# Reading back the expert results: three tiles later in the row queue, and VectorE's last sums held until every scatter has landed

## The chip, the cores and the metric

The kernel runs on one core of one Trainium2 chip. The metric is the device time in microseconds of one execution, lower being better. The core has TensorE (PE in the profile, with weight loads as PEld), VectorE (DVE), ScalarE (ACT), GpSimd (POOL) and SyncE (SP). SP and GpSimd issue the transfers here: SP plain ones, GpSimd those that gather or scatter rows by a list of addresses.

## The reference

A macaron block on 4096 tokens of width 256 (2 x 2048): half a mixture-of-experts step, attention with a convolution ahead of it, and half a mixture-of-experts step again with the same weights. The change touches only the last part.

```
x = x + 0.5 * _L0_ffn_ref(_layernorm(x), gate_up_proj, down_proj, router_w)
x = x + _L0_attn_ref(_layernorm(x), ...)
x = x + 0.5 * _L0_ffn_ref(_layernorm(x), gate_up_proj, down_proj, router_w)

# _L0_ffn_ref: 8 experts, hidden width 176, each token goes to its best two
probs = softmax(h @ router_w.T); vals, idx = top_k(probs, 2); vals = vals / vals.sum()
for each expert:  y = silu(h @ gate.T) * (h @ up.T) @ down.T
                  acc = acc + combine_weight[token, expert] * y
```

## The kernel before

Tokens lie in 32 token tiles of 128. For the expert step, each token's two copies are sorted by expert, and the sorted rows fill 71 expert tiles of 128 rows (`SLOT_TILES`), some of them padding. In the second expert step (`R[1]`) the five engines each run a loop over the expert tiles `s`:

- SP (`load_rows`, L615) loads the 128 rows of tile `s` (129 KB) from DRAM into a ring of four places in `yg`. It issues this when tile `s - 4` has been turned by TensorE and VectorE has read the addresses of tile `s - 4` from the ring (`rowsT`, `dest`).
- TensorE turns the rows (L1842), multiplies by gate and up weights (L1855), turns the hidden rows (L1866, L1867) and multiplies by the down weights (L1875 to L1879). It works two tiles deep: in step `s` it turns tile `s + 1`, does gate and up of `s`, turns hidden `s - 1` and does down of `s - 2`.
- VectorE and ScalarE split values into high and low parts between these; ScalarE copies the result out of PSUM (`y_sb`, L861), and VectorE computes where each row goes (`y_dest`, L1391).
- GpSimd (`send_sums`, L767) scatters the 128 result rows to DRAM (`y_rows`), where the two results of one token are neighbours. The semaphores `st0` to `st3` count the scatters that landed.

Then come the last sums. Token tile `t` becomes x + w0 * y0 + w1 * y1. VectorE does 20 token tiles, two operations each (`last_sum`, L1152, both inputs and the output in SBUF). ScalarE and TensorE do the other 12 (`BY_ACT`, L1064, L1745, L1747, L1069). SP stores the result, two token tiles at a time, in 16 stores of 256 KB (`store_sums`, L637).

The results must be read back from `y_rows`. All results of the first 20 token tiles (`AHEAD`) are in expert tiles below 47 (`AHEAD_FROM`), whatever the routing, because attention's tokens were sorted in two parts. So SP reads those 20 token tiles (256 KB each, `load_ahead`, L623, into buffers that nothing uses any more) while the expert loop still runs: one ahead of the row load of each of the expert tiles 52 to 70, and the last one behind it. Ahead of the first it waits for the scatters below tile 47. The remaining 12 token tiles are read in six transfers of 512 KB into `w_lo` (`load_sums`, L631), when all 71 scatters have landed. SP works its queue strictly in order: a wait ahead of one transfer holds all that stand behind it.

Of the kernel before, what the change touches and what calls it, by code (L numbers as in the profile page):

```python
# [40 lines left out]
SLOT_TILES = (TOPK * TOKENS + E * (P - 1)) // P  # L41
# [31 lines left out]
TAIL_TURN = TILES + 1  # L73
AHEAD_FROM = (TOPK * EARLY_BLOCKS * P + E * (P - 1)) // P
AHEAD = EARLY_BLOCKS
AHEAD_AT = AHEAD_FROM + 5
EARLY_ROUNDS = EARLY // 4


# [27 lines left out]
def macaron_kernel(nc, x, conv_w, conv_b, wq, wk, wvT, wo, bq, bk, bo, proj_w, proj_b, gupT, dpT, rwT,  # L107
                   out, h_dram, y_dram):
    ctx = ExitStack()
    with ctx:  # L110
# [131 lines left out]
        RING = 4  # L242
# [94 lines left out]
        R = [dict() for _ in range(2)]  # L337
# [96 lines left out]
        def in_ring(u):  # L434

            return (SLOT_TILES - u + RING - 1) // RING
# [120 lines left out]
        @block.sync  # L557
        def _(sp):
            for c in range(CHUNKS):
                sp.dma_start(x_view[:, c * CHUNK:(c + 1) * CHUNK, :], x_rows[:, c * CHUNK:(c + 1) * CHUNK, :]  # L560
                             ).then_inc(x_in[c], 16)
                if c == 0:
                    sp.dma_start(rw_sb[:, :], rwT).then_inc(rw_in, 16)
            sp.wait_ge(made, 4)
            for k in range(2):
                for dst, src in w_loads[k]:
                    sp.dma_start(dst, src, allow_slow_non_contiguous=True).then_inc(w_in[k], 16)

            def store_first(groups):
                for g in groups:  # L570
                    sp.wait_ge(first["normed"], GROUP * (g + 1))
                    sp.dma_start(h_dram[g * GROUP * P:(g + 1) * GROUP * P, :].rearrange("(i p) d -> p i d", p=P),
                                 h_rings[g]).then_inc(first[f"stored{g}"], 16)

            store_first((0, 1))
            for dst, src in loads:
                sp.dma_start(dst, src, allow_slow_non_contiguous=True).then_inc(loaded, 16)
            store_first((2, 3))

            pad_regs = [sp.alloc_register(f"pad_at{e}") for e in range(E)]  # L580

            def fill_pad(e):
                if e == 0:
                    sp.wait_ge(T["pads_at"], 1)
                    sp.load(pad_regs, pad_i[0:1, :])
                at = sp.snap(pad_regs[e], min_val=e * REGION, max_val=e * REGION + TOKENS)
                sp.dma_start(h_regions[bass.ds(at, P), :], pad_rows[:, :]).then_inc(T["pads"], 16)

            def load_rows(L):
                r = R[L]  # L590
                regs = [sp.alloc_register(f"rows_at{u}") for u in range(8)]
                for first in range(0, TABLE_TILES, 8):
                    if first in (0, EARLY):
                        sp.wait_ge(T["row_table"], 1 + first // EARLY)
                    sp.load(regs, row_i[0:1, first:first + 8])
                    if first == 0:
                        sp.wait_ge(T["combined"], TILES)
                        for q in range(GROUP):
                            sp.wait_ge(T[f"sent{q}"], 32 * len(range(q, EARLY_BLOCKS, GROUP)))
                    if first == EARLY:  # L600
                        for q in range(GROUP):
                            sp.wait_ge(T[f"sent{q}"], 32 * TILES // GROUP)
                        sp.wait_ge(T["pads"], 16 * E)
                        sp.wait_ge(T["dummies"], 16 * SPARE_TILES)
                    for n in range(min(8, SLOT_TILES - first)):
                        s = first + n
                        if FIRST_PAD <= s < FIRST_PAD + E:
                            fill_pad(s - FIRST_PAD)
                        at = sp.snap(regs[n], min_val=0, max_val=E * REGION + (SPARE_TILES - 1) * P)
                        if AHEAD_AT <= s < AHEAD_AT + AHEAD:  # L610
                            load_ahead(s - AHEAD_AT)
                        if s >= RING:
                            sp.wait_ge(r["rowsT"], s + 1)
                            sp.wait_ge(r["dest"], s - RING + 1)
                        sp.dma_start(rows_in[L][:, s % RING, :], h_regions[bass.ds(at, P), :]  # L615
                                     ).then_inc(r[f"g{s % RING}"], 16)

            def load_ahead(t):

                if t == 0:  # L620
                    for u in range(RING):
                        sp.wait_ge(R[1][f"st{u}"], 16 * len(range(u, AHEAD_FROM, RING)))
                sp.dma_start(ahead_in[t], y_tokens[:, t, :]).then_inc(y_in(t // 2)[0], 16)  # L623

            def load_sums(L):
                for t in range(SLOT_TILES - AHEAD_AT, AHEAD):
                    load_ahead(t)
                for u in range(RING):
                    sp.wait_ge(R[L][f"st{u}"], 16 * in_ring(u))
                for g in range(AHEAD // 2, TILES // 2):  # L630
                    sp.dma_start(y_pairs(g), y_tokens[:, 2 * g:2 * g + 2, :]).then_inc(y_in(g)[0], 16)  # L631

            def store_sums():
                for g in range(TILES // 2):
                    sp.wait_ge(final, sum(t not in BY_ACT for t in range(2 * g + 2)))
                    after(sp, final_act, sum(t in BY_ACT for t in range(2 * g + 2)))
                    sp.dma_start(out_rows[:, 2 * g:2 * g + 2, :], x_view[:, 2 * g:2 * g + 2, :]).then_inc(written, 16)  # L637
                sp.wait_ge(written, 16 * (TILES // 2))

            def store_y(L):  # L640
                r = R[L]

                def store(s, u):
                    sp.wait_ge(r["y_sb"], s + 1 + 2)
                    sp.dma_start(y_dram[bass.ds(s * P, P), :], y_sb[:, u, :]).then_inc(r[f"st{u}"], 16)

                with sp.Fori(0, SPARE_TILES) as j:
                    for u in range(RING):
                        store(RING * j + u, u)
                    sp.dma_start(h_regions[bass.ds(j * P + E * REGION, P), :], pad_rows[:, :]  # L650
                                 ).then_inc(T["dummies"], 16)
                with sp.Fori(0, SLOT_TILES // RING - SPARE_TILES) as j:
                    for u in range(RING):
                        store(RING * j + u + RING * SPARE_TILES, u)
                for s in range(SLOT_TILES // RING * RING, SLOT_TILES):
                    store(s, s % RING)

            sp.wait_ge(loaded, 16 * len(loads))
            sp.wait_ge(first["tokens"], 1)
            sp.dma_start(conv_sb, conv_w).then_inc(loaded, 16)  # L660
            store_y(0)
            for p in range(TILES // 2):
                sp.wait_ge(T["qk"], p + 1)
                sp.dma_start(swapped[W:2 * W, p % 2, :], qk[p % 2][0:W, :]).then_inc(T["swapped"], 16)
                sp.dma_start(swapped[0:W, p % 2, :], qk[p % 2][W:2 * W, :]).then_inc(T["swapped"], 16)
            load_rows(1)
            load_sums(1)

            store_sums()
# [431 lines left out]
        def _(v):  # L1101
            st = Steps(v, dve)
# [38 lines left out]

            def last_sum():
                by_dve = [t for t in range(TILES) if t not in BY_ACT]
                for pair in zip(by_dve[0::2], by_dve[1::2]):
                    done = []
                    for k in range(TOPK):
                        for n, t in enumerate(pair):
                            if k == 0:
                                v.wait_ge(*y_in(t // 2))
                            else:  # L1150
                                v.wait_ge(dve, done[n])
                            ins = v.scalar_tensor_tensor(out=x_tile(t),  # L1152
                                                         in0=y_block(t)[:, k * D:(k + 1) * D],
                                                         scalar=wts[:, k, t:t + 1], in1=x_tile(t),
                                                         op0=ALU.mult, op1=ALU.add)
                            if k == 0:
                                st.did(ins)
                                done.append(st.n)
                            else:
                                ins.then_inc(final, 1)  # L1160
# [1050 lines left out]
```

## Time and profile before

| | |
|---|---|
| time, median of 3 runs | 756.57 us (755.98 to 757.07) |
| the profiled execution's own time | 754.7 us |
| its span in the profile | 752.9 us |
| PE busy | 668.6 us (89%) |
| DVE busy | 522.3 us (69%) |
| ACT busy | 489.9 us (65%) |
| POOL busy | 379.5 us (50%) |
| transfers | 85.50 MB, mean 114 GB/s |

Busy shares are means over stages with different limits. The expert loop of the second step and the last sums, the last 190 us or so, are the part in which the changed lines run; there one reads which engine waits for what, from the timeline and the chain of waits.

### The profile page before, as it was taken

How to read it: one execution, taken by the hardware profiler on the slowest of the kernel's cores; microseconds unless marked ns; L12 is line 12 of the kernel's file. 1: busy time of each engine (PE TensorE's matmuls, PEld its weight loads, DVE VectorE, ACT ScalarE, POOL GpSimd, SP SyncE). 2: the span in 40 equal slices, each digit the busy share in tenths (PEclk: the TensorE clock that was granted, in tenths of full speed). 3: DMA queues.
4: the chain of work that ended last, by engine and by line, in shares of the span. 5: the costliest groups of instructions: out<-in, count | busy, mean ns of one | idle time of the engine just before them, and what ended most of it. 6: DMA issues, size and time to landing. Idle time of an engine off the chain costs nothing. (4 is left out here: it accounts for less than half of the span.)

```text
span 752.9 us, 18893 instructions
## 1 busy us (share of the span) xinstructions
PE 668.6 (89%) x5168; PEld 593.7 (79%) x5169; DVE 522.3 (69%) x1831; ACT 489.9 (65%) x1702; POOL 379.5 (50%) x418
## 2 busy tenths in 40 slices
PE   3999799999997699998898989878688999989974
PEld 3986699999994578887787878767467999979953
DVE  6587566666666467777878777858768677756762
ACT  5775566666664278888877878768444666656653
POOL 4200644444434545666887877563645444434450
PEclk9999899999999689999999999999968999999998
DMA  9930345544442211111222222010223644457619
GB/s 307 311 125 1 109 142 148 146 128 131 130 113 84 84 37 36 41 53 52 78 65 65 66 71 63 30 64 16 93 86 111 180 134 128 128 171 231 190 62 334
DMA packets 60584, 85.50 MB, mean 114 GB/s; under 512 B 10192, under 2 KB 46547, under 8 KB 60500
## 3 DMA queue, kind: packets, MB, share of 16 engines
q1 hardware_dynamic: 47492, 49.73, 21.8%
q0 software_dynamic: 13008, 34.69, 14.8%
q8 instruction: 47, 0.77, 0.5%
q14 instruction: 37, 0.30, 0.2%
HBM read 45.77 MB, written 37.44 MB: 111 GB/s over the span
## 5 line engine op out<-in xcount | busy, mean ns | idle before, releaser
L1855 PE MATMUL CC<-w_hi,turned_parts 128*128 x568 | 176.7, 353 | 2.5 <-DVE turned_parts L1378 2.5
L750 POOL DMA_INDIRECT shared<-h_rows,tok_i x71 | 69.9, 984 | 117.1 <-issue 59.1
L767 POOL DMA_INDIRECT y_rows<-shared,y_dest x71 | 77.7, 1095 | 80.0 <-DVE y_dest L1391 57.5
L1855 PEld LDWEIGHTS CC<-w_hi,turned_parts 128*128 128x128 f32 x568 | 106.8, 195 | 3.3 <-issue 3.2
L843 ACT ACTIVATE shared<-CC 128x176 f32<-128x176 f32 x142 | 45.2, 318 | 78.0 <-PE CC L1855 72.4
L1855 PE MATMUL CC<-w_lo,turned_parts 128*128 x284 | 93.9, 331 | 0.0
L959 ACT ACTIVATE pr<-SS,nmax 128x128 f32<-128x128 f32 x256 | 90.4, 400 | 0.0
L783 POOL TENSOR_TENSOR pr<-pr,prec 128x1024 f32<-128x1024 f32 x31 | 58.9, 1901 | 51.2 <-DVE prec L1614 49.9
L1372 DVE TENSOR_TENSOR shared<-shared,CC 128x176 f32<-128x176 f32 x142 | 47.9, 338 | 50.0 <-ACT shared L843 28.7
L814 POOL DMA_INDIRECT h_regions<-h_store,dest x64 | 65.0, 1015 | 32.7 <-issue 17.2
L791 POOL DMA_INDIRECT yg<-y_rows,slot_i x64 | 62.7, 979 | 34.5 <-DMA y_rows<-shared 15.5
L861 ACT ACTIVATE shared<-SS 128x256 f32<-128x256 f32 x142 | 54.6, 385 | 29.7 <-issue 14.8
L959 ACT ACTIVATION_READ_ACCUMULATOR pr<-SS,nmax 128x1 f32 x256 | 61.7, 241 | 0.0
L950 ACT ACTIVATE shared<-CC 128x512 f32<-128x512 f32 x64 | 34.7, 594 | 33.5 <-PE CC L1997 30.7
L1855 PEld LDWEIGHTS CC<-w_lo,turned_parts 128*128 128x128 f32 x284 | 55.8, 197 | 0.0
L1875 PE MATMUL SS<-w_hi,turned_parts 128*128 x142 | 52.4, 369 | 1.0 <-DVE turned_parts L1385 0.7
L1378 DVE TENSOR_TENSOR turned_parts<-A,turned_parts 128x256 fp32r<-128x256 f32 x68 | 28.9, 425 | 26.4 <-ACT turned_parts L849 26.0
L1378 DVE TENSOR_TENSOR turned_parts<-B,turned_parts 128x256 fp32r<-128x256 f32 x74 | 31.4, 424 | 21.6 <-ACT turned_parts L849 17.8
L1989 PE MATMUL SS<-shared 64*128 64x128 f32 x256 | 38.3, 292 | 5.8 <-DVE shared L1489 4.4
L1584 DVE TENSOR_REDUCE nmax<-SS 128x8 f32<-128x1024 f32 x32 | 39.0, 1219 | 4.6 <-PE SS L1989 4.6
L1989 PEld LDWEIGHTS SS<-shared 64*128 64x128 f32 x256 | 32.1, 194 | 11.2 <-issue 3.0
L1878 PE MATMUL SS<-w_lo,turned_parts 112*128 x142 | 40.7, 287 | 0.0
(404 smaller groups left out, 2108.9 us busy)
## 6 DMA issues: line engine op xcount, KB each, us to landing
yg<-h_regions SPq DMA_DIRECT2D x71, 129.0 KB
y_rows<-shared SPq DMA_DIRECT2D x71, 128.0 KB
x_sb<-in_x_dram SPq DMA_DIRECT2D x8, 512.0 KB, 9.7
out_dram<-x_sb SPq DMA_DIRECT2D x16, 256.0 KB, 6.6
w_lo<-y_rows SPq DMA_DIRECT2D x6, 512.0 KB, 4.2
w_lo<-in_gupT_dram SPq DMA_DIRECT2D x2, 1408.0 KB, 12.4
shared<-tile_oh SPq DMA_DIRECT2D x32, 64.0 KB
h_regions<-pad_rows SPq DMA_DIRECT2D x15, 129.0 KB
```

What stands on the lines that cost most here:

```text
L750: pool.indirect_dma_start(out=rows[:, s % RING, 0:D], out_offset=None, in_=h_dram[:, :], in_offset=bass.IndirectOffsetOnAxis(ap=tok_i[:, s ...
L767: pool.indirect_dma_start(out=y_dram[0:TOPK * TOKENS, :], out_offset=bass.IndirectOffsetOnAxis(ap=y_dest[:, s:s + 1], axis=0), in_=y_sb[:, ...
L783: pool.tensor_tensor(pr[:, q, :, :], pr[:, q, :, :], prec[:, q, :].unsqueeze(2).to_broadcast([P, NH, P]), ALU.mult).then_inc(t["norm"], 1)
L791: pool.indirect_dma_start(out=yg[:, q, k, :], out_offset=None, in_=y_dram[:, :], in_offset=bass.IndirectOffsetOnAxis(ap=slot_i[:, b, k:k + ...
L814: pool.indirect_dma_start(out=h_regions[:, :], out_offset=bass.IndirectOffsetOnAxis(ap=dest[:, q, k:k + 1], axis=0), in_=hr[:, q, :], in_o ...
L861: a.activation(y_sb[:, u % RING, :], SS[:, 512 * (u % 2):512 * (u % 2) + D], ACT.Copy).then_inc(r["y_sb"], 1)
L959: e = a.activation(pr[:, u % 2, h, :], SS[:, h * P:(h + 1) * P], ACT.Exp, bias=nmax[:, u % 2, h:h + 1], accum_out=psums[:, u % 2, h:h + 1])
L1372: v.tensor_tensor(hid[:, p, 0:H], gate[:, p, :], CC[:, 512 * p + H:512 * p + GU], ALU.mult).then_inc(r["hid"], 1)
L1378: v.tensor_tensor(rowsT_lo[:, p, :], rows_turned(r, u), rowsT_hi[:, p, :].bitcast(F32), ALU.subtract).then_inc(r["rowsT_lo"], 1)
L1855: i = pe.matmul(CC[:, 512 * (u % 2):512 * (u % 2) + GU], rows_part[:, u % 2, c * P:(c + 1) * P], weights, start=(n == 1), stop=(n == 3 * DC))
L1875: pe.matmul(acc, hidA_hi[:, u % 2, :], w_hi[:, at_a], start=True, stop=False)
L1989: x = pe.matmul(SS[:, at_h * P:(at_h + 1) * P], heads[lo:lo + KD, m % 2 * 2 + m // 2, :], key_of(i, h % 2), start=False, stop=True, skip_g ...
```

## The change

The 20 reads ahead begin at the row load of expert tile 55 instead of 52, and are spread over the 16 row loads that are left: one ahead of most, two ahead of four of them (of tiles 58, 62, 66 and 70). None is left for after the loop. VectorE's first last sum also waits until all 71 scatters have landed. What is waited for ahead of the first read ahead (the scatters below tile 47) is as before.

```
-AHEAD_AT = AHEAD_FROM + 5
+AHEAD_AT = AHEAD_FROM + 8
...
-                        if AHEAD_AT <= s < AHEAD_AT + AHEAD:
-                            load_ahead(s - AHEAD_AT)
+                        if s >= AHEAD_AT:
+                            for t in ahead_with(s - AHEAD_AT):
+                                load_ahead(t)
...
+            def ahead_with(n):
+
+                steps = SLOT_TILES - AHEAD_AT
+                return range(n * AHEAD // steps, (n + 1) * AHEAD // steps)
+
...
             def load_sums(L):
-                for t in range(SLOT_TILES - AHEAD_AT, AHEAD):
-                    load_ahead(t)
                 for u in range(RING):
                     sp.wait_ge(R[L][f"st{u}"], 16 * in_ring(u))
...
             def last_sum():
                 by_dve = [t for t in range(TILES) if t not in BY_ACT]
+                for u in range(RING):
+                    v.wait_ge(R[1][f"st{u}"], 16 * in_ring(u))
                 for pair in zip(by_dve[0::2], by_dve[1::2]):
```

The first place is SP's queue in the expert loop. L615 is the row load of an expert tile (the ISA row ahead of it carries its waits), L623 the read ahead. Before, the queue around the row loads of tiles 51 to 54 reads so:

```order
L615 ISA [waits r1_dest,r1_rowsT]
L615 DMA yg<-h_regions 128x258
L623 DMA conv_qk_hi<-y_rows 128x512 [waits r1_st2,r1_st3,r1_st1,r1_st0]
L615 ISA [waits r1_dest,r1_rowsT]
L615 DMA yg<-h_regions 128x258
L623 DMA conv_qk_lo<-y_rows 128x512
L615 ISA [waits r1_dest,r1_rowsT]
L615 DMA yg<-h_regions 128x258
L623 DMA pr<-y_rows 128x512
L615 ISA [waits r1_dest,r1_rowsT]
L615 DMA yg<-h_regions 128x258
```

Now the row loads have the line L616 and the reads ahead L629; around the row loads of tiles 54 to 58 it reads:

```order
L616 DMA yg<-h_regions 128x258
L629 DMA conv_qk_hi<-y_rows 128x512 [waits r1_st2,r1_st3,r1_st1,r1_st0]
L616 ISA [waits r1_dest,r1_rowsT]
L616 DMA yg<-h_regions 128x258
L595 TENSOR_LOAD row_i
L629 DMA conv_qk_lo<-y_rows 128x512
L616 ISA [waits r1_dest,r1_rowsT]
L616 DMA yg<-h_regions 128x258
L629 DMA pr<-y_rows 128x512
L616 ISA [waits r1_dest,r1_rowsT]
L616 DMA yg<-h_regions 128x258
L629 DMA conv_v<-y_rows 128x512
L629 DMA pr<-y_rows 128x512
```

The wait on the scatters stood ahead of the row load of tile 52 and stands ahead of that of tile 55; the row loads of 52, 53 and 54 have moved in front of it.

The second place is VectorE's program where the expert loop ends (L1384 and L1385 are its last two operations for an expert tile) and the last sums begin. Before:

```order
L1384 TENSOR_TENSOR turned_parts<-F,turned_parts 128x128 [waits r1_hidT_hi]
L1385 TENSOR_TENSOR turned_parts<-F,turned_parts 48x128
L1152 SCALAR_TENSOR_TENSOR x_sb<-conv_qk_hi,wts,x_sb 128x256 [waits y_in0]
L1152 SCALAR_TENSOR_TENSOR x_sb<-conv_qk_lo,wts,x_sb 128x256 [waits y_in0]
L1152 SCALAR_TENSOR_TENSOR x_sb<-conv_qk_hi,wts,x_sb 128x256 [waits dve]
```

And now:

```order
L1390 TENSOR_TENSOR turned_parts<-F,turned_parts 128x128 [waits r1_hidT_hi]
L1391 TENSOR_TENSOR turned_parts<-F,turned_parts 48x128
L1158 SCALAR_TENSOR_TENSOR x_sb<-conv_qk_hi,wts,x_sb 128x256 [waits r1_st3,r1_st2,y_in0,r1_st1,r1_st0]
L1158 SCALAR_TENSOR_TENSOR x_sb<-conv_qk_lo,wts,x_sb 128x256 [waits y_in0]
L1158 SCALAR_TENSOR_TENSOR x_sb<-conv_qk_hi,wts,x_sb 128x256 [waits dve]
```

Only the first sum has new waits, on the four scatter semaphores; all 40 sums stand behind it. ScalarE's, TensorE's and GpSimd's programs are the same instruction for instruction.

## Rows read from the trace of the kernel before

**Rows 1.** The chain that ended last, in the expert loop: start us, us, what.

```profile
662.99 7.10 issue
670.21 0.34 SPq L623
...
671.05 2.85 DMA yg<-h_regions
```

**Rows 2.** Timeline of PE, the turns of tiles 51, 52, 53, 55 and 70.

```profile
668.22 0.38 PE L1842 MATMUL B<-ident,yg 128*128 128x128 f32 x2
673.95 0.44 PE L1842 MATMUL A<-ident,yg 128*128 128x128 f32 x2 [3.56 <-DMA yg<-h_regions]
676.63 0.63 PE L1842 MATMUL B<-ident,yg 128*128 128x128 f32 x2
...
681.59 0.38 PE L1842 MATMUL B<-ident,yg 128*128 128x128 f32 x2
...
712.04 0.38 PE L1842 MATMUL A<-ident,yg 128*128 128x128 f32 x2
```

**Rows 3.** Busy time by stretch: window, PE, PEld, DVE, ACT, POOL; PEclk, DMA share, GB/s.

```profile
640.00:660.00 20.00, 19.98 (x148) 19.41 (x147) 14.10 (x50) 13.22 (x50) 9.60 (x11) 1.00 0.43 133
660.00:680.00 20.00, 16.44 (x112) 16.09 (x111) 10.79 (x38) 10.12 (x38) 7.41 (x8) 0.91 0.54 174
680.00:700.00 20.00, 19.90 (x149) 19.49 (x148) 14.15 (x49) 13.23 (x50) 9.34 (x10) 1.00 0.80 240
```

**Rows 4.** Timeline of POOL: the scatters of tiles 46, 69 and 70.

```profile
667.76 0.98 POOL L767 DMA_INDIRECT y_rows<-shared,y_dest  x1 [1.03 <-DVE y_dest L1391]
...
718.99 1.07 POOL L767 DMA_INDIRECT y_rows<-shared,y_dest  x1 [0.60 <-issue]
720.37 8.01 POOL L767 DMA_INDIRECT y_rows<-shared,y_dest  x1 [0.30 <-issue]
```

**Rows 5.** Timeline of DVE and of ACT: last sums (ACT: copy of tile 18).

```profile
717.53 0.48 DVE L1152 SCALAR_TENSOR_TENSOR x_sb<-conv_qk_hi,wts,x_sb 128x256 f32<-128x256 f32 x1
...
727.04 0.47 DVE L1152 SCALAR_TENSOR_TENSOR x_sb<-hT_sb,wts,x_sb 128x256 f32<-128x256 f32 x1
729.96 0.38 ACT L1069 ACTIVATE x_sb<-B 128x256 f32<-128x256 f32 x1 [0.29 <-PE B L1747]
733.43 0.48 DVE L1152 SCALAR_TENSOR_TENSOR x_sb<-w_lo,wts,x_sb 128x256 f32<-128x256 f32 x1 [5.92 <-DMA w_lo<-y_rows]
...
741.74 1.27 DVE L1152 SCALAR_TENSOR_TENSOR x_sb<-w_lo,wts,x_sb 128x256 f32<-128x256 f32 x3 [1.51 <-DMA w_lo<-y_rows]
```

**Rows 6.** The chain that ended last, in the tail.

```profile
720.37 9.16 DMA y_rows<-shared,y_dest
...
745.12 0.38 ACT x_sb L1069
```

**Rows 7.** Timeline of DVE and of POOL at 75 us.

```profile
75.33 2.88 DVE L1237 TENSOR_TENSOR w_lo<-w_lo,w_hi 128x960 fp32r<-128x960 f32 x4
...
75.34 3.85 POOL L750 DMA_INDIRECT shared<-h_rows,tok_i  x1 [43.09 <-DVE tok_i L1271]
```

**Rows 8.** SP's queue, timeline: row load of tile 70, and the tail.

```profile
705.64 0.33 SPq L615 DMA_DIRECT2D yg<-h_regions  x1
...
729.67 3.05 SPq L631 DMA_DIRECT2D w_lo<-y_rows  x6
732.76 16.10 SPq L637 DMA_DIRECT2D out_dram<-x_sb  x16
```

**Rows 9.** Busy time by stretch in the tail, columns as in rows 3.

```profile
731.00:739.00 8.00, 3.18 (x14) 2.11 (x12) 3.79 (x10) 3.18 (x8) 0.00 (x0) 1.00 0.94 334
...
743.00:751.00 8.00, 2.09 (x9) 1.46 (x7) 0.01 (x1) 0.77 (x2) 0.00 (x0) 0.93 1.09 382
```

**Rows 10.** DMA queue: packets, MB, share; issues and us to landing, 715 to 753.

```profile
q1 hardware_dynamic: 5984, 7.34, 54.6%
...
out_dram<-x_sb SPq DMA_DIRECT2D x16, 256.0 KB, 6.6
```

## The prediction

> **What bounds the kernel now.** I read the chain of waits first, because two places in it are no work of any engine. The first is in the expert loop: 7.10 us without an instruction from 662.99, then SP's first read ahead at 670.21, then the row load of tile 52 at 671.05, which lands 2.85 us later [rows 1]. That is SP standing ahead of the first read ahead until the scatter of tile 46 has landed, with the row load of tile 52 behind it. The timeline of TensorE shows what it costs. Tile 52 should be turned 2.0 us after tile 51, and is turned 5.73 us after it, with TensorE idle for 3.56 us on the row load [rows 2]. The window around it has TensorE busy for 16.44 of 20 us, where its neighbours have 19.98 and 19.90; its granted clock is 0.91 instead of 1.00 [rows 3]. So outside this stall TensorE bounds the loop, at one tile per 2.03 us: (712.04 - 681.59) / 15 [rows 2].
>
> The second is behind the loop. The scatter of tile 69 occupies GpSimd for 1.07 us, that of tile 70 for 8.01 us, from 720.37 to 728.38 [rows 4]. It lands 9.16 us after its start [rows 6], and only then, at 729.67, does SP issue the first read into w_lo [rows 8]. In the same time VectorE does its sums on the data read ahead without a gap, from 717.53 to 727.51, and then idles 5.92 us [rows 5]. From 731 on the transfers are the bound: 334 GB/s up to 739 and 382 GB/s from 743 to 751, at a busy share of 0.94 and 1.09, with every compute engine mostly idle [rows 9]. The traffic there is 7.34 MB [rows 10], six reads of 512 KB and 16 stores of 256 KB. At 382 GB/s it is 19.2 us, of the 23.2 between the first issue and the end of the span (752.9 - 729.67).
>
> So two delays are in series. What the loop saves arrives whole at the tail, since all 71 scatters must land before SP goes on.
>
> **Part 1: reads ahead from tile 55.** The wait itself is unchanged: the scatter of tile 46 starts at 667.76 [rows 4] and SP is released at 670.21 [rows 1], 2.45 us later, in the new kernel too. What moves is what stands behind it. The row loads of 52, 53 and 54 go out when their own waits allow. Tile 55 becomes the first one held. A row load that nothing holds goes out 6.4 us before its tile is turned (tile 70: 705.64 [rows 8] and 712.04 [rows 2]). TensorE, without a stall, turns tile 55 at 668.22 + 4 x 2.03 = 676.3, so its row load is wanted at 669.9. SP gets to it at about 671.05, as it got to tile 52 now, and its rows land 2.85 us later, at 673.9 [rows 1]. There are 2.4 us to spare, so the stall is gone and no new one takes its place.
>
> What that is worth: from the turn of tile 51 to that of tile 55 pass 681.59 - 668.22 = 13.37 us now [rows 2], and four steps take 8.1. The gain is 5.3 us: some 3.7 of waiting, and the rest from steps at the lower clock behind the pause (tile 52 to 53 takes 2.68 us), which goes with the pause. The lower bound, if the clock dips anyway, is 3.6 us.
>
> The cost is density. 20 reads of 256 KB go into 16 steps; now 19 go into 19. One read ahead per step raised the busy share of the transfer engines from 0.43 to 0.80 [rows 3], so one is worth 0.37. Five in four steps make 0.43 + 1.25 x 0.37 = 0.89. A step with two has 1.17, which is 0.17 x 2.03 = 0.35 us of backlog, gone in the next two steps. A row load behind two reads ahead instead of one lands some 0.8 us later (256 KB more, at the 334 GB/s of rows 9), so in 3.7 us instead of 2.85, against the 6.4 us that it has. I take 0 us for it, with up to 1.5 us in the range: at four steps the backlog could show on TensorE.
>
> The twentieth read ahead moves from behind the last row load to ahead of it. It is one more issue on SP (0.34 us [rows 1]), with 6.4 us before tile 70 is turned: 0.
>
> **Part 2: VectorE waits for the scatters.** The question is whether the sums are why the last scatter takes 8.01 us. The release fits: the scatter ends at 728.38, 0.87 us behind the end of the sums at 727.51, and 0.98 is what the scatter of tile 46 takes [rows 4, 5]. At 75 us there is a second such case: the first gather starts at 75.34, with VectorE's four subtractions between SBUF tensors from 75.33 to 78.21, and ends at 79.19, 0.98 us behind them [rows 7]. Against it stands the scatter of tile 69, which runs from 718.99 amid the same sums and takes only 1.07 us.
>
> The Trainium skill (SBUF — State Buffer, Who interferes with whom) says that a VectorE instruction with two SBUF inputs contends with a GpSimd instruction that reads SBUF, and that the loser waits for one instruction to end. Read strictly, the scatter would lose one sum of 0.48 us, not 7. The same page's warning on "DVE blocks DMA" says that GpSimd cannot write descriptors while VectorE holds the port pair. By the first the 8 us would have another cause and part 2 would gain nothing; by the second it gains what is worked out below. This trace agrees with the second at two places and with the first at the scatter of tile 69.
>
> I go by the two cases in which GpSimd's operation ends 0.9 to 1.0 us behind VectorE's run. Without the sums, the scatter of tile 70 starts at 720.3 as now (that of 69 sheds 0.1), takes 0.98 us, and lands 2.45 us after its start, as that of tile 46 did [rows 1, 4]. SP then issues the first read of w_lo at 722.7 instead of 729.67: 7.0 us earlier.
>
> VectorE begins its sums at 722.7 instead of 717.53, 5.2 us later, and all 40 stand behind the wait. Each takes 0.40 us (727.51 - 717.53 for 25 of them [rows 5]), so they end at 722.7 + 16 = 738.7, if w_lo is there. It is: the first is needed after 26 sums, at 733.1. ScalarE and TensorE do not wait, and are done with the token tiles read ahead at 730.3, as now [rows 5].
>
> What SP does next: it issues six reads (3.05 us), then stores as token tiles become final, at one per 16 / 16 = 1.0 us from 724.3 on. The reads (3.15 MB at 334 GB/s [rows 9]) fill the transfer engines until 722.7 + 9.4 = 732.1, when eight stores are ready behind them, and at 0.7 us a store (256 KB at 382 GB/s) the backlog lasts until the sums are over. The transfers stay the bound, so the tail behind the first read keeps its 23.2 us: 722.7 + 23.2 = 745.9, against 752.9. Gain 7.0 us. If the first 8 us ran at 382 instead of 334 GB/s, 1.0 us would go too: a gain of 8.0. If stores come too thinly while the reads run, 1 us is lost: a gain of 6.0.
>
> **Sum.** 5.3 + 7.0 = 12.3 us. The profiled execution took 754.7 us with a span of 752.9; less 12.3, 742.4 with a span of 740.6. The median shown is 1.87 us above that execution: 756.57 - 12.3 = 744.3 us.
>
> **Rivals.**
>
> *Only the loop gains.* VectorE's sums cost a scatter no more than one of them, 0.1 to 0.5 us as at tile 69, and the last scatter is slow for another reason, such as something in GpSimd's own end of the loop. (This is what the sentence of the Trainium skill, SBUF — State Buffer, on two SBUF inputs comes to; the trace agrees with it at tile 69 alone.) Then w_lo is read from 729.67 less 5.3 as now, and VectorE starts at that moment too: it ends 16 us later, at 745.7 on the old scale, about when ScalarE is done now (745.5 [rows 6]), so the stores lose little; I give them 0.5 us. 756.57 - 5.3 + 0.5 = 751.8 us. For it speaks the scatter of tile 69; against it two ends that follow VectorE's by 0.9 us. 4 in 100.
>
> *The loop gains little.* The denser reads ahead hold up row loads at the four double steps, or SP's queue backs up. Each lost step is 0.5 to 1 us plus the clock behind it; four of them cost 2 to 4 us. 756.57 - 12.3 + 3 = 747.3 us. For it: a busy share of 0.89 with a backlog at double steps. Against it: 6.4 us of lead against 3.7, and only 0.1 us of TensorE lost in 20 with one read ahead per step [rows 3]. 12 in 100.
>
> *Slower than before.* VectorE's sums become the bound of the tail. Held until 722.7 and then run beside full transfers, they take a time q each; the last store goes out behind the last sum and lands 6.6 us later [rows 10]: 722.7 + 40 q + 6.6 against 752.9 + 5.3. It decides from q = 0.72 us. At q = 0.85 the end is 763.3 less 5.3, that is 758.0, and the time 756.57 + 5.1 = 761.7 us. Against it: the three sums from 741.74, amid full transfers, take 1.27 us, 0.42 each [rows 5]. 2 in 100.
>
> *The change does nothing.* For that SP would have to be held at tile 55 as at 52, with the scatter of tile 46 landing well over 2.4 us later than now, and the last scatter would have to be slow as well: 756.6 us, 1 in 100.
>
> **How the numbers follow.** My forecast has 81 in 100: 744.3, its range from the bounds above. Down: 1.0 us for transfers at full rate, and 1.3 for steps of the loop that are not perfectly even now (TensorE has 19.90 of 20 [rows 3]) and the spread of runs, gives 742.0. Up: 1.5 for the backlog and 1.0 for thin stores give 746.8, or 1.7 if the clock dips anyway; the range goes to 747.8, so that it holds the second rival's centre. What is left out is below 742.0, the worse half of the second rival, and the others. A measurement of this kernel tells a difference from 0.2% (1.5 us) on. Faster by more than that are the forecast and the first two rivals, 0.97 or so; within it the last, 0.01; slower 0.02.
>
> **What the profile of the changed kernel would show.** Part 1: TensorE turns tiles 51 to 55 at an even 2.0 us, the 660 to 680 window has about 19.9 us of TensorE and a clock of 1.00, and the chain has no 7 us gap in the loop. SP's row loads of 52 to 54 come 2 us apart, and the next is near 671. If part 1 is wrong, an idle time of TensorE on the row load stands at tile 55 or behind a double step. Part 2: no scatter above 1.1 us; the last one lands about 2.4 us after its start, and VectorE's first sum and SP's first read of w_lo begin together, at about 717.4 on the new scale (722.7 - 5.3). The transfers then run above 330 GB/s to the end, and VectorE has no idle time on w_lo longer than 2 us. If the scatter takes 8 us again with VectorE idle, my cause is wrong. If the rate between 719 and 728 stays well under 330 GB/s, the stores are too thin and the tail is bound by the sums.

## The result, and the profile after

The changed kernel takes 746.72 us (median of 7 runs, 743.28 to 749.49), against 756.81 us for the kernel before in the same comparison (7 runs). The ratio is 0.9869, with a 95% interval of 0.9837 to 0.9901. Single runs of either kernel scatter by 5 to 6 us. The two profiled executions have spans of 752.9 and 741.1 us, 11.8 us apart; they are one execution each, and that of the changed kernel (743.28 us) is the fastest of its seven, so the difference of the spans says no more about the gain than the medians do. What the two traces are good for is to compare the parts that changed.

The timeline of TensorE shows the turns of tiles 51 to 55 and of tile 70, answering to [rows 2]:

```profile
668.12 0.38 PE L1848 MATMUL B<-ident,yg 128*128 128x128 f32 x2
670.14 0.38 PE L1848 MATMUL A<-ident,yg 128*128 128x128 f32 x2
672.15 0.39 PE L1848 MATMUL B<-ident,yg 128*128 128x128 f32 x2
674.62 0.43 PE L1848 MATMUL A<-ident,yg 128*128 128x128 f32 x2 [0.30 <-issue]
676.70 0.38 PE L1848 MATMUL B<-ident,yg 128*128 128x128 f32 x2
...
707.38 0.38 PE L1848 MATMUL A<-ident,yg 128*128 128x128 f32 x2
```

Tile 51 is turned within 0.1 us of where it was, so from there on the two traces can be laid side by side. Four steps take 8.58 us instead of 13.37. Tile 70 is turned 4.66 us earlier. By stretch, as in [rows 3]:

```profile
660.00:680.00 20.00, 19.70 (x146) 19.30 (x146) 14.14 (x49) 12.98 (x48) 9.25 (x10) 1.00 0.63 194
680.00:700.00 20.00, 19.70 (x148) 19.32 (x147) 14.28 (x50) 13.24 (x50) 9.83 (x10) 1.00 0.89 278
```

TensorE has lost its idle time on the row load and its dip of the granted clock (1.00 instead of 0.91). The transfer engines are denser, 0.89 busy where they were 0.80.

SP's timeline shows where the stall was that it still makes, and the tail ([rows 1, 8]):

```profile
670.21 0.34 SPq L629 DMA_DIRECT2D conv_qk_hi<-y_rows  x1
671.01 0.10 SPq L616 DMA_DIRECT2D yg<-h_regions  x1
...
717.90 3.04 SPq L635 DMA_DIRECT2D w_lo<-y_rows  x6
720.99 16.45 SPq L641 DMA_DIRECT2D out_dram<-x_sb  x16
```

The first read ahead goes out at 670.21, to the hundredth as before. It is now ahead of the row load of tile 55, which goes out at 671.01 and is not missed: tile 55 is turned at 676.70.

GpSimd's last two scatters, and VectorE's last sums ([rows 4, 5]), from the timelines:

```profile
714.33 0.98 POOL L771 DMA_INDIRECT y_rows<-shared,y_dest  x1 [0.60 <-issue]
715.62 0.99 POOL L771 DMA_INDIRECT y_rows<-shared,y_dest  x1 [0.30 <-issue]
```

```profile
717.93 0.48 DVE L1158 SCALAR_TENSOR_TENSOR x_sb<-conv_qk_hi,wts,x_sb 128x256 f32<-128x256 f32 x1 [5.10 <-DMA y_rows<-shared,y_dest]
...
728.63 5.23 DVE L1158 SCALAR_TENSOR_TENSOR x_sb<-w_lo,wts,x_sb 128x256 f32<-128x256 f32 x13
```

The last scatter takes 0.99 us instead of 8.01. VectorE pays for that with 5.10 us of idle time and then does all 40 sums without a gap. By stretch in the tail, as in [rows 9]:

```profile
721.00:727.00 6.00, 6.00 (x26) 4.55 (x27) 6.00 (x16) 5.02 (x13) 0.00 (x0) 1.00 0.92 311
727.00:731.00 4.00, 3.99 (x18) 2.80 (x17) 4.00 (x11) 3.33 (x8) 0.00 (x0) 1.00 1.06 380
731.00:739.00 8.00, 1.48 (x6) 0.97 (x6) 2.85 (x8) 0.77 (x2) 0.00 (x0) 0.85 1.09 383
```

The transfers are full from 727 on. Between 721 and 727 they are not quite, and SP's own waits say why: it now waits 7.3 us in all, 11 times, for VectorE's sums ahead of a store (before: 2.5 us, 5 times).

```profile
SPq L633 <- DMA y_rows<-shared,y_dest: 16.4, 1, 16.4
SPq L641 <- DVE x_sb L1158: 7.3, 11, 1.1
```

### The profile page after: what moved, and what is told of

Its sections match the earlier page's. It is cut to its first block and busy times, and to the rows that moved or that the text cites. A ratio compares the mean times of both kernels' runs of the same rounds, so it can differ in the third digit from the quotient of the medians.

```text
span 741.1 us, 18895 instructions
## 1 busy us (share of the span) xinstructions
PE 663.7 (90%) x5168; PEld 589.3 (80%) x5169; DVE 521.2 (70%) x1831; ACT 488.4 (66%) x1702; POOL 372.2 (50%) x418
## 5 line engine op out<-in xcount | busy, mean ns | idle before, releaser
L771 POOL DMA_INDIRECT y_rows<-shared,y_dest x71 | 70.5, 993 | 75.5 <-DVE y_dest L1397 57.4
L1881 PE MATMUL SS<-w_hi,turned_parts 128*128 x142 | 52.2, 368 | 1.0 <-DVE turned_parts L1391 0.7
L1384 DVE TENSOR_TENSOR turned_parts<-B,turned_parts 128x256 fp32r<-128x256 f32 x74 | 31.3, 423 | 21.1 <-ACT turned_parts L853 17.0
L1384 DVE TENSOR_TENSOR turned_parts<-A,turned_parts 128x256 fp32r<-128x256 f32 x68 | 28.8, 424 | 24.0 <-ACT turned_parts L853 23.7
L1883 PE MATMUL SS<-w_hi,turned_parts 128*128 x142 | 40.4, 285 | 0.0
```

The source lines that it names most:

```text
L771: pool.indirect_dma_start(out=y_dram[0:TOPK * TOKENS, :], out_offset=bass.IndirectOffsetOnAxis(ap=y_dest[:, s:s + 1], axis=0), in_=y_sb[:, ...
L1384: v.tensor_tensor(rowsT_lo[:, p, :], rows_turned(r, u), rowsT_hi[:, p, :].bitcast(F32), ALU.subtract).then_inc(r["rowsT_lo"], 1)
L1881: pe.matmul(acc, hidA_hi[:, u % 2, :], w_hi[:, at_a], start=True, stop=False)
L1883: pe.matmul(acc, hidA_lo[:, u % 2, :], w_hi[:, at_a], start=False, stop=False)
```

## The experiments

Executions differ by some microseconds in the long part ahead of the last expert loop, and both kernels can come out 2% faster in one group of runs than in another: the kernel before took 740.84 us beside experiments 1 to 4, 756.93 beside 5, 6, 7 and 11, 740.39 beside 8 and 9, and 755.59 beside 10. So each ratio is against the kernel before in the same group, and places in a trace are compared within that trace unless a shared point is named. Edits are to the changed kernel unless said otherwise.

**1. The reads ahead alone.**

```
             def last_sum():
                 by_dve = [t for t in range(TILES) if t not in BY_ACT]
-                for u in range(RING):
-                    v.wait_ge(R[1][f"st{u}"], 16 * in_ring(u))
```

> Only the reads ahead are changed; VectorE's sums begin at once, as before. Theory (two delays in series): the loop's stall goes, the last scatter still takes about 8 us and ends 0.9 us behind VectorE's run of 25 sums; the span is 752.9 - 4.7 = 748 us, the time about 5 us less than before. Rival (the late reads themselves freed the last scatter, since fewer transfers compete near the end): the last scatter takes 1 us, and the time is 10 us less than before.

Measured: ratio 0.9931 (0.9906 to 0.9955), 735.69 against 740.84 us. The last scatter in the timeline of POOL, and VectorE's last sum on the data read ahead:

```profile
698.00 8.01 POOL L771 DMA_INDIRECT y_rows<-shared,y_dest  x1 [0.31 <-issue]
```

```profile
704.68 0.47 DVE L1156 SCALAR_TENSOR_TENSOR x_sb<-hT_sb,wts,x_sb 128x256 f32<-128x256 f32 x1
```

It takes 8.01 us again, and ends 0.86 us behind the sums (706.01 and 705.15). No turn of a tile waits for its rows in this trace. So the loop's gain stands by itself, and later reads do not free the last scatter.

**2. VectorE's wait alone**, added to the kernel before.

```
             def last_sum():
                 by_dve = [t for t in range(TILES) if t not in BY_ACT]
+                for u in range(RING):
+                    v.wait_ge(R[1][f"st{u}"], 16 * in_ring(u))
```

> Only VectorE's wait is added; the reads ahead begin at tile 52 as before. Theory: TensorE idles 3.6 us on the row load of tile 52 as before, the last scatter takes 1.0 us and SP's first read of w_lo comes 7.0 us earlier than in the kernel before; the time is 7 us less than before. Rival (the sums do not hold the scatter): the scatter takes 8 us still, with VectorE idle, and the time is 0 to 1 us more than before.

Measured: ratio 0.9917 (0.9887 to 0.9946), 734.12 against 740.84 us. PE's timeline has tiles 51, 52 and 53, POOL's the last scatter:

```profile
650.92 0.38 PE L1844 MATMUL B<-ident,yg 128*128 128x128 f32 x2
656.57 0.63 PE L1844 MATMUL A<-ident,yg 128*128 128x128 f32 x2 [3.47 <-DMA yg<-h_regions]
660.19 0.38 PE L1844 MATMUL B<-ident,yg 128*128 128x128 f32 x2
```

```profile
703.05 0.99 POOL L767 DMA_INDIRECT y_rows<-shared,y_dest  x1 [0.30 <-issue]
```

The stall at tile 52 is whole, the scatter is free. With VectorE idle it takes 0.99 us, so GpSimd's own end of the loop is not what made it long.

**3. The changed kernel beside the two halves.** No edit.

> The changed kernel again, beside the two halves on one chip. Theory: its gain is the sum of the gains of the two halves, 11.8 us by the spans of the two profiled executions. Rival (the halves overlap, since the median of the first timing moved by only 10.1 us): the gain is 2 us or more below the sum of the halves.

Measured: ratio 0.985 (0.9814 to 0.9885), 729.18 against 740.84 us. The halves saved 0.69% and 0.83%, which is 1.52%, and both together 1.50%, or 11.1 us of 740.84. So they add up. Each interval is some 2 us or more to either side, as much as the rival's difference, so the times alone would not refuse the rival. The traces help: with the late reads in both, the last scatter starts at the same time with and without VectorE's wait (698.00 in experiment 1, 698.03 here), and SP's first read of w_lo comes 7.0 us apart. In SP's timeline, experiment 1 and then this run:

```profile
707.30 3.02 SPq L635 DMA_DIRECT2D w_lo<-y_rows  x6
```

```profile
700.30 3.08 SPq L635 DMA_DIRECT2D w_lo<-y_rows  x6
```

**4. Reads ahead from tile 53.**

```
-AHEAD_AT = AHEAD_FROM + 8
+AHEAD_AT = AHEAD_FROM + 6
```

> The changed kernel with the reads ahead begun at tile 53, 20 reads over 18 row loads. Theory (what stands behind the wait on the scatter of tile 46 gets out at 671.05 and its rows land at 673.9): tile 53 would be turned at 672.2, so TensorE idles 1.7 us on it, and with some lower clock behind it the time is 2 to 3 us more than with tile 55. Rival (one tile later is enough, since an idle time under 2 us costs nothing on the clock and the loop has slack): no idle time above 0.5 us, the time as with tile 55.

Measured: ratio 0.9868 (0.9833 to 0.9902), 731.21 us, 2.0 us more than the changed kernel beside it, by medians; the intervals overlap. The trace shows the stall. PE's timeline, tiles 52, 53 and 54:

```profile
657.27 0.38 PE L1848 MATMUL A<-ident,yg 128*128 128x128 f32 x2
660.88 0.44 PE L1848 MATMUL B<-ident,yg 128*128 128x128 f32 x2 [1.44 <-DMA yg<-h_regions]
663.14 0.44 PE L1848 MATMUL A<-ident,yg 128*128 128x128 f32 x2
```

TensorE idles for 1.44 us on tile 53, against 1.7 expected. The row load behind the wait lands at a fixed time, and each tile's delay of the wait buys one step of 2.0 us: 3.5 us of idle time at tile 52, 1.4 at 53. The expected loss in clock did not come: the window from 650 to 670 has a granted clock of 1.00.

**5. Reads ahead from tile 54.**

```
-AHEAD_AT = AHEAD_FROM + 8
+AHEAD_AT = AHEAD_FROM + 7
```

> The changed kernel with the reads ahead begun at tile 54, 20 reads over 17 row loads. Theory: the rows of tile 54 land at 673.9 and are needed at 674.3, so TensorE idles at most 0.5 us and the time is that of the changed kernel within 0.5 us. Rival (the third tile is needed too): an idle time of 1 us or more at tile 54 and 2 us more.

Measured: ratio 0.9845 (0.9815 to 0.9875). Tile 54 is turned without waiting for its rows; PE's timeline has tiles 53, 54 and 55:

```profile
671.62 0.39 PE L1848 MATMUL B<-ident,yg 128*128 128x128 f32 x2
673.92 0.43 PE L1848 MATMUL A<-ident,yg 128*128 128x128 f32 x2
675.99 0.38 PE L1848 MATMUL B<-ident,yg 128*128 128x128 f32 x2
```

No idle time is named, and the step of 2.30 us is no longer than the one of 2.47 at the same tile with the wait one tile later. By the trace two tiles would have done, and the third is a reserve.

**6. What in the sums holds the scatter?** The time in which VectorE waits now was filled with 20 operations of the sums' kind. Their results are read by nobody; the output is unchanged. The first fill has a constant as its multiplier:

```
             def last_sum():
                 by_dve = [t for t in range(TILES) if t not in BY_ACT]
+                filled = []
+                for n in range(20):
+                    if n >= 2:
+                        v.wait_ge(dve, filled[n - 2])
+                    st.did(v.scalar_tensor_tensor(out=(zeros[:, :], best_flat)[n % 2],
+                                                  in0=w_hi[:, 0:D].bitcast(F32), scalar=1.0,
+                                                  in1=w_hi[:, D:2 * D].bitcast(F32), op0=ALU.mult, op1=ALU.add))
+                    filled.append(st.n)
                 for u in range(RING):
```

(`best_flat` stands for the tile `best` as 128x256.)

> The changed kernel, and in the 5 us in which VectorE waits for the scatters it does 20 operations of the sums' kind (multiply and add, 128x256, both inputs in SBUF) whose results nobody reads; they take 8 us. Theory (an unbroken run of VectorE operations with two SBUF inputs holds a scatter): the last scatter takes about 5 us, ends about 0.9 us behind the twentieth operation, near 721.7, and the time is 4 us more than the changed kernel's. Rival (it was the real sums' use of x or of the read-ahead buffers, or GpSimd's own end of loop): the last scatter takes 1 us and the time grows by less than 1 us.

Measured: the theory, as it was put, falls. The fill runs from 712.78 to 719.57 without a gap, and the last two scatters pass through it:

```profile
714.24 1.16 POOL L771 DMA_INDIRECT y_rows<-shared,y_dest  x1 [0.60 <-issue]
715.71 1.04 POOL L771 DMA_INDIRECT y_rows<-shared,y_dest  x1 [0.30 <-issue]
```

They are delayed by 0.18 and 0.06 us against the 0.98 us of a scatter beside an idle VectorE, and not held until the fill ends. The two filling operations that were running when they started are these:

```profile
714.13 0.42 DVE L1152 SCALAR_TENSOR_TENSOR zeros<-w_hi 128x256 f32<-128x256 f32 x1
...
715.47 0.42 DVE L1152 SCALAR_TENSOR_TENSOR zeros<-w_hi 128x256 f32<-128x256 f32 x1
```

The ratio is 0.9811 (0.9773 to 0.9849), no worse than without the fill. An unbroken run with two tensor inputs in SBUF does not by itself hold a scatter to its end.

**7. The same with the second input in PSUM**: `in1=CC[:, 0:D]`.

> The same 20 operations, with the second input from PSUM instead of SBUF; nobody reads the results. Theory (it is the second SBUF input that holds GpSimd): the last scatter takes 1.0 us, SP's first read of w_lo comes near 717.9, VectorE's sums start 3 us late, and since the transfers bound the tail the time grows by 0 to 2 us. Rival (any unbroken VectorE run holds the scatter): as with both inputs in SBUF, the scatter ends 0.9 us behind the run and the time is 4 us more than the changed kernel's.

Measured: ratio 0.984 (0.9802 to 0.9878), time as the changed kernel's within the noise. Its only profiled execution took 1213 us, so nothing rests on its trace. The time does not tell anything apart by itself, since the fill with both inputs in SBUF did not hold the scatter either.

**8 and 9. What the real sums have beside two tensors in SBUF.** The real multiplier is a column of `wts` in SBUF, and the real sum is written over its own second input. Each was tried alone in the fill of experiment 6.

```
-                                                  in0=w_hi[:, 0:D].bitcast(F32), scalar=1.0,
+                                                  in0=w_hi[:, 0:D].bitcast(F32), scalar=wts[:, 0, 0:1],
```

> As the run that filled the wait with 20 operations on two SBUF inputs, but the multiplier is a column of wts in SBUF, as in the real sums, instead of a constant. (The 20 results are read by nobody.) Theory A (it is the multiplier read from SBUF that holds GpSimd, or the longer operation that it makes): the last scatter ends about 0.9 us behind the twentieth operation, near 721.6, having taken 5 to 6 us. Theory B (it is the sum written over its own input): the scatter takes 1.0 to 1.2 us.

```
-                                                  in1=w_hi[:, D:2 * D].bitcast(F32), op0=ALU.mult, op1=ALU.add))
+                                                  in1=(zeros[:, :], best_flat)[n % 2], op0=ALU.mult, op1=ALU.add))
```

> As the run that filled the wait with 20 operations on two SBUF inputs, constant multiplier kept, but the second input is the tile that is written, as in the real sums. (The 20 results are read by nobody.) Theory A (the multiplier from SBUF): the last scatter takes 1.0 to 1.2 us. Theory B (written over its own input): it ends about 0.9 us behind the twentieth operation, near 720, having taken 4 to 5 us.

Measured, the last two scatters of the run with the multiplier in SBUF, the filling operations that were running when they started, and the last filling operation:

```profile
701.74 1.07 POOL L771 DMA_INDIRECT y_rows<-shared,y_dest  x1 [0.60 <-issue]
703.12 6.03 POOL L771 DMA_INDIRECT y_rows<-shared,y_dest  x1 [0.30 <-issue]
```

```profile
701.48 0.48 DVE L1152 SCALAR_TENSOR_TENSOR best<-w_hi,wts 128x256 f32<-128x256 f32 x1
...
703.06 0.48 DVE L1152 SCALAR_TENSOR_TENSOR best<-w_hi,wts 128x256 f32<-128x256 f32 x1
...
707.81 0.48 DVE L1152 SCALAR_TENSOR_TENSOR best<-w_hi,wts 128x256 f32<-128x256 f32 x1
```

And the last scatter of the run that writes over its input:

```profile
701.83 1.04 POOL L771 DMA_INDIRECT y_rows<-shared,y_dest  x1 [0.30 <-issue]
```

Both came out as theory A has it. With the multiplier in SBUF the last scatter takes 6.03 us and ends 0.86 us behind the fill (709.15 and 708.29), the distance seen with the real sums; the ratio is 0.9928 (0.9898 to 0.9958). Written over its own input, with a constant, the fill does not hold it, ratio 0.9847 (0.9819 to 0.9876). So the hold can be made again with operations that touch neither x nor the read-ahead buffers. These two runs and the next rest on two or three executions and one trace each.

**10. Multiplier in SBUF, second tensor in PSUM.** The fill of experiment 6 with `scalar=wts[:, 0, 0:1]` and `in1=CC[:, 0:D]`.

> The 20 filling operations once more (their results are read by nobody), with the multiplier from SBUF, one tensor input from SBUF and the other from PSUM. Theory A (it takes two tensor inputs in SBUF and the multiplier in SBUF together): the last scatter takes 1.0 to 1.2 us. Theory B (the multiplier in SBUF is enough, whatever the tensors): it ends 0.9 us behind the twentieth operation, having taken about 6 us.

Measured: ratio 0.9836 (0.9787 to 0.9885), as theory A has it. Here are operations of the fill and the last two scatters:

```profile
712.62 0.47 DVE L1152 SCALAR_TENSOR_TENSOR best<-w_hi,wts,CC 128x256 f32<-128x256 f32 x1
...
713.80 0.47 DVE L1152 SCALAR_TENSOR_TENSOR zeros<-w_hi,wts,CC 128x256 f32<-128x256 f32 x1
714.19 0.47 DVE L1152 SCALAR_TENSOR_TENSOR best<-w_hi,wts,CC 128x256 f32<-128x256 f32 x1
```

```profile
712.89 0.98 POOL L771 DMA_INDIRECT y_rows<-shared,y_dest  x1 [0.59 <-issue]
714.18 0.98 POOL L771 DMA_INDIRECT y_rows<-shared,y_dest  x1 [0.31 <-issue]
```

These operations start every 0.39 us, as the real ones do (0.40), where those with a constant start every 0.34. So the pace alone does not hold a scatter.

**What experiments 6 to 10 leave open: when the scatter starts.** The fills differ in more than what was written into them. A scatter starts at some point of the VectorE operation that is then running, and that point moves with the pace of the run and with how long the scatter ahead of it took. In the kernel before, these operations were running when the scatters of tiles 69 (718.99) and 70 (720.37) started:

```profile
718.73 0.48 DVE L1152 SCALAR_TENSOR_TENSOR x_sb<-conv_qk_lo,wts,x_sb 128x256 f32<-128x256 f32 x1
...
720.31 0.48 DVE L1152 SCALAR_TENSOR_TENSOR x_sb<-wvo_hi,wts,x_sb 128x256 f32<-128x256 f32 x1
```

The same reading of the traces, in us, wherever VectorE is in a gapless run when both scatters start:

| run | tile 69 starts behind the operation's start | takes | tile 70 starts behind the operation's start | takes |
|---|---|---|---|---|
| before | 0.26 | 1.07 | 0.06 | 8.01 |
| 1, real sums | 0.27 | 1.07 | 0.05 | 8.01 |
| 8, two tensors and multiplier in SBUF | 0.26 | 1.07 | 0.06 | 6.03 |
| 6, constant multiplier | 0.11 | 1.16 | 0.24 | 1.04 |
| 9, constant, written over its input | 0.11 | 1.17 | 0.24 | 1.04 |
| 10, one tensor in PSUM | 0.27 | 0.98 | 0.38 | 0.98 |

All three scatters that were held started 0.05 or 0.06 us behind the start of an operation, and none of the others closer than 0.11. The gather at 75 us, held for 3.85 us, started 0.01 us behind the first of VectorE's four operations (75.34 and 75.33, [rows 7]). So a rival to "the multiplier in SBUF" fits every row: two tensors in SBUF, a run without gaps, and a start close behind that of an operation. It would also say why tile 69 escapes beside the very same operations, and why the gather is held by operations that have no multiplier, and neither follows from the multiplier. (In the 1213 us execution of experiment 7 the last scatter starts 0.03 us behind an operation with one tensor in PSUM and takes 0.98 us, which the rival allows.) No run changed the starting point alone: the constant changes the pace (0.34 instead of 0.40), and with one tensor in PSUM the scatter of tile 69 takes 0.98 us instead of 1.07, so that tile 70 starts at another point. The test would be a fill with a constant multiplier, shifted until the last scatter starts 0.06 us behind an operation. What the table does show, at one and the same starting point (tile 69, 0.26 to 0.27), is that three reads of SBUF delay a scatter by 0.09 us, and one tensor in PSUM takes that away.

**11. Four sums ahead of the wait, and their store.** A version meant to use the idle stretch.

```
             def load_sums(L):
+                store_sum(0)
                 for u in range(RING):
                     sp.wait_ge(R[L][f"st{u}"], 16 * in_ring(u))
...
-                for u in range(RING):
-                    v.wait_ge(R[1][f"st{u}"], 16 * in_ring(u))
                 for pair in zip(by_dve[0::2], by_dve[1::2]):
+                    if pair[0] == 3:
+                        for u in range(RING):
+                            v.wait_ge(R[1][f"st{u}"], 16 * in_ring(u))
```

> The changed kernel, but VectorE does the four sums of token tiles 0 and 1 before it waits for the scatters, and SP stores them before it waits. Theory (a short run of sums that is over before the last scatter starts at 715.6 does not hold it): the four sums lie at 712.8 to 714.5, the last scatter takes 1.0 us, and one store of 256 KB moves into the idle stretch, so the transfer-bound tail is 0.7 us shorter. Rival (four sums already delay the scatter of tile 69 and all behind it): the last scatter lands 1 us later and the time is 0.3 to 1 us more.

Measured: ratio 0.9835 (0.9803 to 0.9868), 743.96 us, beside 744.49 for the reads from tile 54 in the same group: no difference that these runs can tell. The trace has what the theory says:

```profile
715.85 0.41 SPq L641 DMA_DIRECT2D out_dram<-x_sb  x1
719.26 2.97 SPq L636 DMA_DIRECT2D w_lo<-y_rows  x6
```

```profile
716.99 0.98 POOL L775 DMA_INDIRECT y_rows<-shared,y_dest  x1 [0.30 <-issue]
```

The store goes out 3.4 us ahead of the reads, the last scatter takes 0.98 us, and 22.6 us lie between the first read and the end of the span (741.9 - 719.26), where the four traces with an unchanged tail (the changed kernel, experiments 3, 4 and 5) have 23.2 to 23.7. That is in line with the 0.7 us expected, from one trace.

## Why the prediction was right, step by step

The forecast was 744.3 us, and 12.3 us less than before; measured were 746.72 us, 10.1 us less by medians and 11.8 by the spans. Experiment 3 gave 1.50% or 11.1 us. All lie inside the range and somewhat short of the forecast. The prediction took 0.2% for what a measurement of this kernel tells; the interval came out as 0.3% to either side.

- **The loop's stall**: 5.3 us forecast, 4.66 measured at the turn of tile 70. The mechanism was as told: SP released at 670.21, tile 55 not waiting, no dip of the clock. What the sum missed is that a step is not always 2.03 us. The changed kernel has a step of 2.47 us at tile 54, with a pause that the profile puts down to "issue" and not to a transfer. With reads from tile 54 there is one of 2.30 at the same place. Such a longer step comes at every eighth tile (in the changed kernel 38, 46, 54 and 62; in the kernel before 38, 46 and 62, with 54 inside the slow stretch), and nearly all the others take 2.01 us. The 2.03 of the prediction is the mean of both kinds, and the four steps held one of the long ones.
- **Density**: 0 us forecast, with a busy share of 0.89; 0.89 was measured from 680 to 700, and no turn waits for its rows. It may not have been quite free: from tile 55 to 70 the loop takes 30.68 us instead of 30.45, and of these 0.23 us the longer step at tile 62 has 0.19 (2.47 instead of 2.28). At tile 46, ahead of any read ahead, that step takes 2.14 and 2.16 us. At tile 62 it takes 2.38 us in experiment 2, where the reads ahead are as before, so part of the 0.19 is spread. That denser transfers lengthen it is a guess that no run tested.
- **The last scatter**: 7.0 us forecast. The first read of w_lo comes 11.77 us earlier, of which 4.66 are the loop's: 7.11. The landing was put at 2.45 us behind the start, and is 2.3 (717.93 - 715.62).
- **The tail behind the first read**: to stay 23.2 us; it is 741.1 - 717.90 = 23.2. The transfers start a little thinner (311 GB/s from 721 to 727, 325 from 719 to 728), since SP waits for sums, and end at the same rate. That the sums would not bind was nearly but not wholly so. The profile's chain runs through 15.53 us of them, but it stops at 733.9, 7.2 us before the span ends, so it does not settle this. Experiment 10 says more: its fill held the sums until 2.8 us behind the first read of w_lo (719.28 and 716.45), and the tail behind that read took 24.05 us, 0.9 more than 23.2, of which up to 0.5 may be the spread (the unchanged tail took 23.2 to 23.7 us in four traces).
- **Signs that did not come as told**: the steps of tiles 51 to 55 are not an even 2.0 us (2.47 at tile 54), and TensorE has 19.70 us from 660 to 680 instead of 19.9. "No scatter above 1.1 us" was too strict: one early in the loop, at 575.66, takes 1.58 us, as in the kernel before. It is not in the tail.
- **The cause of the 8 us**, weighed at one place against the Trainium skill (SBUF — State Buffer, Who interferes with whom): halving the change shows that the sums are the cause (experiments 1 and 2). The forecast rested on two cases in which GpSimd ends behind a gapless run of VectorE between SBUF tensors; experiment 6 shows that this was too wide a reason. That did no harm to the number, since the change takes away all the sums, and with them any of the narrower reasons. The Trainium skill's sentence on two SBUF inputs, with a wait for one operation at most, fits the fill with a constant multiplier (1.04 and 1.16 us) and the scatter of tile 69. It does not fit the real sums, which held a scatter for some 18 of them, from 720.37 to their end at 727.51 [rows 4, 5]. The Trainium skill's warning (same page) on "DVE blocks DMA", by which the prediction had its gain, is written for VectorE operations in a two-port performance mode; the prediction left this condition out, and no row here shows the mode of these sums.

Still open is what in the run holds one scatter and lets the one before it through: the multiplier in SBUF, or where in an operation the scatter starts, or both. Tile 69 (1.07 us before, in experiment 1 and in experiment 8) and the gather at 75 us ([rows 7], again 3.85 us in the changed kernel) speak for the starting point, and no run was made on either. What was found is for this operation and size alone.

## What to carry to other kernels

A wait ahead of one transfer in an in-order queue is paid by the transfer behind it. Work out when that one is needed, and move the wait back by as many tiles as cover the difference, which is worth whole steps at first and then nothing. An engine that starts its epilogue early can hold up the last transfer that everything waits for: look for a scatter or gather that ends a fixed time behind another engine's run, and let that engine idle for a few microseconds. Where two delays are in series, each half of the change can be timed alone, and here the halves added up. When an experiment changes how fast an engine works, check in the trace whether it has also changed what meets what.

## What the runs showed of the hardware that was not expected

- A scatter issued by GpSimd took 0.98 us beside an idle VectorE. Beside a gapless run of VectorE's multiply-add with both tensors in SBUF it took 1.04 to 1.17 us with a constant multiplier (experiments 6 and 9). With the multiplier in SBUF, one took 1.07 us and the next 6.03 or 8.01 us (before, experiments 1 and 8). It took 0.98 us when one of the tensors came from PSUM (experiment 10). When held, it ended 0.86 to 0.87 us behind VectorE's run, three times out of three.
- The three held scatters started 0.05 or 0.06 us behind the start of a VectorE operation, the others 0.11 us or more. Whether that or the multiplier is the condition is open.
- The multiplier from SBUF also makes the operation itself slower: one every 0.39 to 0.40 us instead of every 0.34 (128x256, f32).
- TensorE's granted clock fell behind a pause of 3.5 us (a mean of 0.91 and 0.92 in the window of 20 us, before and in experiment 2; 0.56 from 676 to 679 in the kernel before, so mostly at the lower of its two levels, 1.2 GHz). It stayed at 1.00, or 2.4 GHz, in the windows with a pause of 1.4 us (experiment 4) and with none.
